# Rows of V ahead of W, divisions apart from their products, the last output tile in halves, and the last w2 split ahead

## The reference

```
x = x + gnn(layernorm(x), edges)      # two graph attention layers, 41250 edges
x = x + ffn(layernorm(x))             # below
# ffn:
y = x + attention(layernorm(x)*g1+b1) # Wqkv (768 x 2304), 12 heads of 64, softmax over 1250 keys, Wproj
out = y + moe(layernorm(y)*g2+b2)     # router 768 -> 8, top 2; expert: gelu(x @ W1[e]) @ W2[e], 768 -> 384 -> 768
```

## Time and profile before

| | |
|---|---|
| median of 3 runs | 1548.36 us (1548.1 to 1548.82) |
| profiled execution | 1550.1 us, span of its instructions 1548.2 us |
| PE busy | 1419.0 us, 92% of the span |
| DVE, ACT, POOL busy | 75%, 63%, 32% |
| PE in the chain that ended last | 70% of the span, DVE 8% |
| mean granted TensorE clock | 0.963 of full |

### The profile page before, as it was taken

One profiled execution on the slowest core, in us unless ns is written; L12 is line 12 of the kernel. 1 busy time (PEld: TensorE's weight loads), 2 busy tenths in 40 slices (PEclk: granted clock), 3 DMA queues, 4 the chain that ended last, 5 costly groups with the idle time before them and its releaser, 6 DMA issues.

```text
span 1548.2 us, 25663 instructions
## 1 busy us (share of the span) xinstructions
PE 1419.0 (92%) x8981; PEld 1344.2 (87%) x8981; DVE 1154.7 (75%) x1751; ACT 971.3 (63%) x1657; POOL 497.1 (32%) x367
## 2 busy tenths in 40 slices
PE   3998799999799979999999999999998998699996
PEld 1897578999699979899898998989988897699996
DVE  6788889735789752486878868778688787788884
ACT  7997787422478322366847668487686521599994
POOL 2000000000000010244626546255465510288885
PEclk9999799999899989999999999999999998799998
DMA  7001000121214540000000000000000495476651
GB/s 199 1 1 40 2 20 17 56 104 58 102 59 154 178 128 1 1 21 1 7 14 0 20 0 0 20 0 0 20 11 21 131 296 148 124 158 160 160 103 23
DMA packets 52312, 99.09 MB, mean 64 GB/s; under 512 B 10848, under 2 KB 26852, under 8 KB 52224
## 3 DMA queue, kind: packets, MB, share of 16 engines
q1 hardware_dynamic: 40848, 75.68, 15.7%
q0 software_dynamic: 11376, 22.29, 7.5%
HBM read 67.15 MB, written 44.31 MB: 72 GB/s over the span
## 4 chain that ended last, share of the span: by engine, by line
PE 70%; DVE 8%; issue 3%; ACT 1%; DMA 1%; POOL 1%; POOLq 0%; DVEq 0%; ACTq 0%
PE ps L372 14%; PE ps L373 14%; PE ps L374 14%; PE ps L823 4%; PE ps L864 4%; PE ps L843 3%; PE ps L866 3%; PE ps L865 3%; PE ps L845 3%; DVE mcol L1066 2%; PE ps L1245 1%; PE ps L598 1%; DVE prlo L1035 1%; PE ps L832 1%; PE ps L1667 1%
## 5 line engine op out<-in xcount | busy, mean ns | idle before, releaser
L1035 POOL TENSOR_TENSOR prlo<-prob,prhi 125x500 fp32r<-125x500 f32 x180 | 249.4, 1391 | 275.2 <-ACT prob L976 274.0
L1066 DVE TENSOR_REDUCE mcol<-ps 125x1 f32<-125x1250 f32 x120 | 175.0, 1458 | 78.5 <-PE ps L823 78.0
L974 ACT ACTIVATE prhi<-ps 125x500 fp32r<-125x500 f32 x300 | 177.0, 590 | 76.6 <-PE ps L845 71.4
L864 PE MATMUL ps<-prhi,vhi 125*128 125x250 f32 x600 | 173.4, 289 | 10.6 <-DVE prlo L1035 4.9
L976 ACT ACTIVATE prob<-ps 125x500 f32<-125x500 f32 x300 | 176.2, 587 | 2.1 <-DVE prlo L1035 2.0
L1521 POOL MEMSET q<- 128x2500 f32 x1 | 2.2, 2188 | 527.4 <-PE ps L374 527.4
L866 PE MATMUL ps<-prlo,vhi 125*128 125x250 f32 x600 | 169.0, 282 | 0.0
L865 PE MATMUL ps<-prhi,vlo 125*64 125x250 f32 x600 | 168.1, 280 | 0.0
L1667 PE MATMUL ps<-ohs,ohd 128*125 128x417 bf16 x380 | 125.8, 385 | 39.5 <-DVE ohs L2092 36.7
L843 PE MATMUL ps<-qst,kst 128*125 128x250 f32 x600 | 156.9, 285 | 3.4 <-issue 1.4
L372 PE MATMUL ps<-hhi,pthi 125*125 125x384 f32 x400 | 152.8, 382 | 3.0 <-DVE ptlo L712 3.0
(11 more groups left out here) (327 smaller groups left out, 4048.2 us busy)
## 6 DMA issues: line engine op xcount, KB each, us to landing
w1all<-in_L_ffn_W_dram SPq DMA_DIRECT2D x8, 1152.0 KB, 9.5
w2st<-in_L_ffn_W_dram SPq DMA_DIRECT2D x8, 1152.0 KB
wqst<-in_L_ffn_Wqkv_dram SPq DMA_DIRECT2D x12, 384.0 KB, 4.2
hid_d<-tin SPq DMA_DIRECT2D x10, 375.0 KB
hin<-hid_d SPq DMA_DIRECT2D x10, 375.0 KB
vtin<-xn_d SPq DMA_DIRECT2D x10, 375.0 KB
out_dram<-accr POOLq DMA_DIRECT2D x10, 375.0 KB, 8.3
xall<-in_x_dram SPq DMA_DIRECT2D x5, 672.0 KB
```

Of the source, the lines that this page charges most:

```text
L864: pe.matmul(ps[:, b:b + GQ], vhi[:, e, kt, :], hi, start=kt == 0, stop=False)
L974: act.activation(prhi[:, n % RING, :], bank(3 + n % 3, P, 2 * GQ), ACT.Exp, scale=float(HD) ** -0.5)
L1035: eng.tensor_tensor(prlo[:, n % RING, :], prob[:, n % 3, :], prhi[:, n % RING, :].bitcast(f32), ALU.subtract)\
L1066: dve.tensor_reduce(mcol[:, e, t:t + 1], ps[0:P, 0:N], AX.X, ALU.max, negate=True).then_inc(sem("max"), 1)
```

## The change

It has five edits; the line numbers of the rows below are those of the kernel before.

1. SP: `v_in(6)` and `v_in(7)` stand ahead of the wait for the last results and of `load_qk(0)`.
2. wqlo of the first pair is made by DVE in two instructions, between v_lower(8) and v_lower(9), and no longer by POOL in one.
3. Last pair: `inverse` of a group is done at units (10, 14, 20) of head 0 and (1, 5) of head 1, `quotients` two units later; before, both were done at (12, 16, 21) and (2, 5).
4. Last output tile: xnr, its turn, ythi, ytlo and the router's steps go in two halves of 384 columns.
5. Experts: in the last turn but one ACT does the w2 split first, ahead of the row and the gelu.

```diff
-        LAST_AT = ((12, 16, 21), (2, 5))
+        LAST_AT = ((10, 14, 20), (1, 5))
...
+                def apart(at, first):
+                    steps = {j: lambda g=g: inverse(p, g + first, True) for g, j in enumerate(at)}
+                    steps.update({j + 2: lambda g=g: quotients(p, g + first, True) for g, j in enumerate(at)})
+                    return steps
...
             def turn(t):
-                pe.wait_ge(sem("n2_row"), t + 1)
+                if t == T - 1:
+                    pe.wait_ge(sem("n2_row"), T)
+                else:
+                    pe.wait_ge(sem("n2_row"), t + 1)
                 if t >= 1:
                     pe.wait_ge(sem("rows_lo"), t)
                 for k in range(KD):
+                    if t == T - 1 and k == KD // 2:
+                        last.then_inc(sem("tile_raw"), 1)
+                        pe.wait_ge(sem("n2_row"), T + 1)
...
-                pe.wait_ge(sem("rows_lo"), t + 1)
+                if t == T - 1:
+                    pe.wait_ge(sem("tile_lo"), 3 * T + 3)
+                else:
+                    pe.wait_ge(sem("rows_lo"), t + 1)
                 for k in range(KD):
+                    if t == T - 1 and k == KD // 2:
+                        pe.wait_ge(sem("rows_lo"), t + 1)
...
             g2_rows(T - 1)
+            v_in(6)
+            v_in(7)
             for n in ("x1", "xa", "xn"):
                 sp.wait_ge(sem(f"{n}_out"), 32 * T)
             load_qk(0)
-            for t in range(6, T):
+            for t in range(8, T):
                 v_in(t)
...
-            split_qk(0)
             pool.wait_ge(sem("v_row"), T)
...
                 if i + 2 < TILES:
                     split_w1(i + 2)
+                elif i + 1 < TILES:
+                    split_w2(i + 1)
                 if i >= 1:
                     row(i - 1)
                 if i + 1 < TILES:
                     gelu(i + 1)
                 if i + 2 < TILES:
                     x_hi(i + 2)
+                    split_w2(i + 1)
                 if i + 1 < TILES:
-                    split_w2(i + 1)
                     ht_hi(i + 1)
...
                 if t + 2 < T:
                     v_affine(dve, t + 2)
+                elif t == T - 2:
+                    lower_qk(dve, 0, 0)
+                    lower_qk(dve, 0, 1)
...
+                for a, b in ((0, HALF), (HALF, D)) if t == T - 1 else ((0, D),):
+                    order.did(dve.scalar_tensor_tensor(xnr[:, u, a:b], accr[:, u, a:b], stat[:, u, 0:1], row2[:, 0, a:b],
+                                                       ALU.subtract, ALU.mult))
```

More of the change, by code:

```diff
@@ L1036, in lower_part, with lower_qk @@
                 .then_inc(sem(done), 1)
+        def lower_qk(dve, p, m):
+            dve.wait_ge(sem("wq_hi"), p + 1)
+            last = dve.tensor_tensor(wqlo[:, m, :, :], wqst[:, m, :, :], wqhi[:, m, :, :].bitcast(f32), ALU.subtract)
+            if m == 1:
+                last.then_inc(sem("wq_lo"), 1)
         def attention_dve(dve, order):
@@ L1114, in head @@
                         steps[j]()
[L1116 to L1120, removed]
             def turn(p, both):
-                head(p, 0, (p, 1), {LOWER_QK_AT[m]: lambda m=m: lower_qk(p + 1, m) for m in range(2)},
+                head(p, 0, (p, 1), {LOWER_QK_AT[m]: lambda m=m: lower_qk(dve, p + 1, m) for m in range(2)},
                      lambda g: outputs(p, 0, g))
@@ L1139, in last_turn @@
             def last_turn(p):
[L1141 to L1145, removed]
+                def apart(at, first):
+                    steps = {j: lambda g=g: inverse(p, g + first, True) for g, j in enumerate(at)}
+                    steps.update({j + 2: lambda g=g: quotients(p, g + first, True) for g, j in enumerate(at)})
+                    return steps
+                head(p, 0, (p, 1), apart(LAST_AT[0], 0), lambda g: outputs(p, 0, g))
                 outputs(p, 0, NG - 1)
-                steps = {j: lambda g=g: both(g + 3) for g, j in enumerate(LAST_AT[1])}
+                steps = apart(LAST_AT[1], 3)
                 steps.update({j: lambda t=t: o_lo(dve, t) for t, j in enumerate(O_LO_AT)})
@@ L1436, in _ @@
                     residual_in(t + 2)
[L1437 removed]
+                sp.wait_ge(sem("n2_row"), t + 1 if t < T - 1 else T + 1)
                 for a, b in CUTS:
@@ L1490, in _ @@
             pool.sem_inc(sem("wq_lo"), 1)
[L1492 to L1495, removed]
             def set_v(p, e, part):
@@ L1887, in _, with last_hi @@
             leave(act, "scalar")
+            def last_hi():
+                act.wait_ge(sem("logit_raw"), T - 1)
+                act.wait_ge(sem("tile_raw"), 3 * T + 3)
+                act.activation(ythi[:, 0:3, :], bank(0, 128, 3 * P).rearrange("p (k c) -> p k c", k=3), ACT.Copy)\
+                    .then_inc(sem("tile_hi"), 1)
+                act.wait_ge(sem("rows_raw"), T)
+                act.activation(ythi[:, 3:KD, :], bank(1, 128, 3 * P).rearrange("p (k c) -> p k c", k=3), ACT.Copy)\
+                    .then_inc(sem("rows_hi"), 1)
             def y_hi(t):
@@ L1907, in _ @@
                     o_hi(act, t + 2)
-            y_hi(T - 1)
+            last_hi()
             act.wait_ge(sem("route_dve"), GAP)
@@ L2270, in y_lo, with last_lo @@
                     .then_inc(sem("rows_lo"), 1)
+            def last_lo():
+                dve.wait_ge(sem("tile_hi"), 3 * T + 1)
+                dve.tensor_tensor(ytlo[:, 0:3, :], bank(0, 128, 3 * P).rearrange("p (k c) -> p k c", k=3),
+                                  ythi[:, 0:3, :].bitcast(f32), ALU.subtract).then_inc(sem("tile_lo"), 1)
+                dve.wait_ge(sem("rows_hi"), T)
+                dve.tensor_tensor(ytlo[:, 3:KD, :], bank(1, 128, 3 * P).rearrange("p (k c) -> p k c", k=3),
+                                  ythi[:, 3:KD, :].bitcast(f32), ALU.subtract).then_inc(sem("rows_lo"), 1)
             def top(t):
@@ L2289, in normed @@
                     dve.wait_ge(sem("rows_raw"), t - 1)
-                order.did(dve.scalar_tensor_tensor(xnr[:, u, :], accr[:, u, :], stat[:, u, 0:1], row2[:, 0, :], ALU.subtract, ALU.mult))
-                order.wait()
-                dve.scalar_tensor_tensor(xnr[:, u, :], xnr[:, u, :], stat[:, u, 2:3], row2[:, 1, :], ALU.mult, ALU.add)\
-                    .then_inc(sem("n2_row"), 1)
+                for a, b in ((0, HALF), (HALF, D)) if t == T - 1 else ((0, D),):
+                    order.did(dve.scalar_tensor_tensor(xnr[:, u, a:b], accr[:, u, a:b], stat[:, u, 0:1], row2[:, 0, a:b],
+                                                       ALU.subtract, ALU.mult))
+                    order.wait()
+                    dve.scalar_tensor_tensor(xnr[:, u, a:b], xnr[:, u, a:b], stat[:, u, 2:3], row2[:, 1, a:b], ALU.mult, ALU.add)\
+                        .then_inc(sem("n2_row"), 1)
             dve.wait_ge(sem("route_act"), WR_HI)
@@ L2306, in _ @@
                     o_lo(dve, t + 2)
-            y_lo(T - 1)
+            last_lo()
             top(T - 2)
```

## The result

The changed kernel takes 1531.46 us (median of 4 runs, 1527.66 to 1534.92) against 1548.59 for the kernel before: ratio 0.9886, 95% interval 0.9874 to 0.9897, 17.1 us less. The forecast was 1530.3, in a range of 1526 to 1536.5. The profiled execution took 1530.46 us with a span of 1528.7; before it was 1550.1 and 1548.2, so the two traces stand 19.5 us apart.

What follows compares the result with a forecast made beforehand. TensorE, busy 92% of the span, was taken as the bound, so edits shorten its waits. Parts of 9.0 + 4.4 + 1.6 + 3.1 = 18.1 us off the median gave 1530.3 us; own range 1527 to 1533.5, wide range 1526 to 1536.5.

Steps and rivals of the forecast that it cites:

- Part 1: V stage: rows 6 and 7 ahead of W; 10.9 us less waits of 0.65 and 1.3 gives 9.0 us.
- Part 2: Last pair: divisions two units ahead of their products; 4.4 us, between 0 and 6.5.
- the term of head 0: Last pair, head 0: products leave the front of the maximum PE waits for; 1.1 us, bounds 0 and 2.8.
- 1.85 + 1.5: Last pair, head 1: 1.85 us less PE wait for the low half, 1.5 us from no lower clock behind it.
- rival (b): Last pair: DVE has no pause, so apart is no faster than together; part 2 gives 0: 1534.7 us; chance 0.17.
- no wait of PE for prlo over 1 us: Expected sign in head 1 of the last pair: PE never waits over 1 us for that low half.
- Part 3: Last output tile: in halves, the first router matmul comes some 1.7 us after PE's turn; 1.6 us taken.
- Part 4: End of experts: w2 split ahead cuts PE's last wait from 2.81 to 1.2 us; 3.1 us, between 1.6 and 3.1.
- its term of clock: End of experts: the lower clock behind PE's last wait would not come; 1.5 us.
- Rival (a): V stage: W behind the rows holds up ACT, xthi of tile 6 and PE; part 1 gives about 4: 1535.3; chance 0.15.
- (c): V stage: row 6 lands no earlier, only DVE's 3.92 us becomes 0.95; 3.0 us gained: 1536.3; chance 0.06.
- (d): V stage: W lands far later, after about 584 us, making the kernel slower than before; chance 0.02.

Runs made afterwards that it cites:

- the second chip: The changed kernel unaltered, measured again on another chip beside the kernel before: 1535.28 us, ratio 0.9919.
- both finds: Changed kernel with V rows in transfers of 112 and 13 rows and head 1's second division behind unit 6: 1534.44 us, ratio 0.9918 to the kernel before.

## Why the prediction was right

**Part 1, V stage, 9.0 us: right by its steps.** Corrected by the 1.0 us that this trace is late, tile 6 turned at 557.5 after 0.2 us of wait (forecast 558.0, 0.65) and tile 8 at 566.5 after 1.21 (forecast 566.9, 1.3), with wqhi at 561.4 (forecast 561.7); the stage gave 9.4, 9.2, 9.0 and 8.5 us in the four executions that have both of its edits and rows in one transfer. Both waits were the price of rows sent in one transfer (0.32 of the DMA engines busy): with rows in two transfers they vanished, and the stage gave 10.9, the bound. wqlo cost nothing, as reckoned. What I did not see is that the earlier trace rows shows one draw. In five more executions with this stage unedited it was 0.1 to 2.2 us shorter, 1.0 in the mean, and the wait for the late row 6.6 to 8.0 us. Against their mean the part is worth 8.0 to 8.4 us in the changed kernel's two traces; alone it gave 7.8.

**Part 2, last pair, 4.4 us: right in mechanism, the term of head 0 too small.** Head 1 gave 3.3 us for 1.85 + 1.5. The wait fell to 0.85 us and not to 0.4, so 1.4 instead of 1.85, and the stretch of lower clock behind it, 3.4 us at half speed, was worth 1.7. Head 0 gave 3.0 for 1.1: TensorE's longest wait for a maximum fell from 2.79 to 1.2 us, 1.6 instead of 1.1, and the rest is the second stretch of lower clock (there was one behind this wait too, 3.4 us long), which I charged to head 1 alone. Together 6.3 in the trace; alone 5.7 (3.4 to 7.0) by the medians. The rule behind rival (b) is true here in every instance that I looked at (products at 1.48 and 1.39 us instead of 0.41), yet the rival fell: behind the held products stands a division, and TensorE waits 0.85 us for the low half after it. Early and together they cost 6 us. The sign "no wait of PE for prlo over 1 us" in head 1 did not hold: the 1.6 us near its end stood before as well, and nothing in the change reaches them.

**Part 3, last tile, 1.6 us: right in the sum, by two terms that miss in opposite ways.** 1.6 in the stage alone, 1.9 with the others, where the lower clock also began at another point. From the turn to the first router matmul the forecast was 1.75 us instead of 3.46, and it took 2.19, alone and with the others, so 1.3 and not 1.7 come from there. The other 0.3 is the turn itself, which in the kernel with this part alone follows route(8) with no wait, 0.3 us earlier than before; the forecast named that limit (1305.0) and counted nothing for it.

**Part 4, W2, 3.1 us: right, but its term of clock is not in every execution.** 3.1 in the trace by the span, 3.2 by the last yrow there and alone; 1.17 us of wait (forecast 1.2) and no lower clock behind it. Of the eight traces with the old order, seven have a stretch of lower clock behind that wait, and the one with the last tile alone has none after 2.8 us; of the six with the new order none has. So 1.65 us are sure and the 1.5 come in most executions; the median alone is 2.7.

**The sum.** 18.1 us were forecast, and the edited stages gave 20.7 in the profile. The median moved by 17.1, and by 13.2 on the second chip, where 1535.28 is outside the forecast's own range (1527 to 1533.5) and inside the wide one. So the forecast of 1530.3 is near in part by luck, for reasons that partly cancel: part 2 gave 1.9 us more, and the median holds less than the trace, because the profiled execution of before was a slow one in the V stage and because the changed kernel loses time in the experts in some executions. I had subtracted only the 1.74 us between its time and the median. Rival (a), W behind the rows, and (c) and (d) are ruled out by wqhi at 562.37 and row 6 at 556.42.

**Open:** whether the changed kernel meets the slow writes oftener than the one before. Two kernels without most of its edits meet them as often as it does, which speaks against it, but no kernel except the changed one has more than one trace. The changed kernel's runs spread over 7.3 and 3.4 us in the two measurements, those of before over 1.1 and 1.6 beside them; but on the other two chips before spread over 5.2 and 6.7.

## What to carry to other kernels

Where an engine's queue feeds two consumers, look at the longest run of instructions that nothing may interrupt: with the divisions at the same early places, products two units later gained 5.7 us and products at once lost 6.2. Find out what the other engine runs beside a two-input VectorE instruction before giving it a place. A wait that one profile shows is one draw; read it in two or three executions before subtracting it, and a longest wait in a list has a place that only the timeline tells.

## What the runs showed that I had not expected

- A VectorE instruction with two SBUF inputs ended 0.81 or 0.82 us after GpSimd's wqlo in seven executions, with durations from 2.20 to 3.92 us. A division (one SBUF input) beside GpSimd's low halves or its split of wproj kept its 1.70 to 1.73 us.
- The lower clock comes and goes between executions in stages with the same instructions. From 649.3 to 656.2 us it held in the trace before; in that stretch of pair 0, 6 of the 13 later executions have none of it and are 2.1 us shorter there. The window of before, and one as long in the kernel with both finds, which takes in the same work:

```profile
649.50:656.00 6.50, 5.65 (x23) 5.17 (x24) 2.41 (x3) 5.01 (x10) 3.64 (x4) 0.50 0.00 0
```

```profile
637.00:643.50 6.50, 4.60 (x35) 4.10 (x34) 2.64 (x3) 6.46 (x12) 5.44 (x4) 1.00 0.00 0
```

- GpSimd's issue of one indirect write took 1.57 us or 3.67 us in the same stage of the same kernel.
